# A written table of steps for the 64-wide attention, its value products taken in pairs, its key tiles in reverse

## What is computed

```python
h = _rms(x, ln_w)
q = (h @ wq).reshape(B, S, 32, 64)
k = (h @ wk).reshape(B, S, 8, 64)
v = (h @ wv).reshape(B, S, 8, 64)
q, k = _rope(q, k)
scores = jnp.einsum('bqhd,bkhd->bhqk', q, repeat(k)) / 8.0
scores = jnp.where(causal, scores, -1e30)
attn = jax.nn.softmax(scores, -1)
o = jnp.einsum('bhqk,bkhd->bqhd', attn, repeat(v))
x = x + o @ wo
```

## Time and profile before

| | |
|---|---|
| median of 3 runs | 2234.08 us (2233.0 to 2237.5) |
| profiled execution | 2239.73 us |
| its span in the trace | 2237.9 us |
| PE busy | 1923.3 us, 86% of the span |
| DVE, ACT, POOL busy | 1292.1, 1080.4, 905.6 us |
| 64-wide attention, all rounds | 842 to 1862 us of the span |

### The profile page before, as it was taken

One profiled execution on the slowest core, in us unless ns is written; L12 is line 12 of the kernel. 1 busy time (PEld: TensorE's weight loads), 2 busy tenths in 40 slices (PEclk: granted clock), 3 DMA queues, 4 the chain that ended last, 5 costly groups with the idle time before them and its releaser, 6 DMA issues.

```text
span 2237.9 us, 37392 instructions
## 1 busy us (share of the span) xinstructions
PE 1923.3 (86%) x11178; PEld 1217.4 (54%) x11178; DVE 1292.1 (58%) x3257; ACT 1080.4 (48%) x2758; POOL 905.6 (40%) x1013
## 2 busy tenths in 40 slices
PE   4979899778787739999999999999999996599995
PEld 2656778533333325666666666666666665455552
DVE  5775453457568466666666666666666665822222
ACT  3324342345455416665566556656665663144442
POOL 4990000022120004444444444444444443468884
PEclk9989899769999979999999999999999997799997
DMA  4000020000000100000000000000000003545556
GB/s 143 1 1 1 9 49 1 1 1 1 1 13 26 39 2 1 1 0 0 0 0 0 0 0 0 0 0 0 0 0 0 0 0 111 206 70 82 84 83 160
DMA packets 61350, 60.76 MB, mean 27 GB/s; under 512 B 13136, under 2 KB 58320, under 8 KB 61264
## 3 DMA queue, kind: packets, MB, share of 16 engines
q0 software_dynamic: 15360, 20.98, 5.9%
q1 hardware_dynamic: 45904, 38.65, 5.4%
HBM read 40.48 MB, written 19.14 MB: 27 GB/s over the span
## 4 chain that ended last, share of the span: by engine, by line
PE 62%; DVE 14%; issue 11%; ACT 7%; POOL 4%; DMA 2%; SPq 0%; ACTq 0%; DVEq 0%; POOLq 0%
PE banks L1804 8%; PE banks L1827 7%; PE banks L1836 6%; PE banks L1815 5%; PE banks L1846 4%; PE banks L1900 3%; PE banks L2024 2%; PE banks L1858 2%; ACT wide_x L1468 2%; PE banks L1875 2%; POOL wdT L751 2%; PE banks L1649 2%; ACT wugT L1482 2%; PE banks L1920 2%; PE banks L1942 1%
## 5 line engine op out<-in xcount | busy, mean ns | idle before, releaser
L1051 DVE TENSOR_REDUCE con<-banks 128x1 f32<-128x256 f32 (+3 forms) x512 | 250.3, 489 | 147.9 <-PE banks L1806 141.1
L1804 PE MATMUL banks<-wide_k,wide_q 128*128 128x512 f32 (+3 forms) x1024 | 300.9, 376 | 0.5 <-ACT wide_k L1419 0.5
L683 POOL TENSOR_TENSOR wugT<-wugT,con 128x512 f32<-128x512 f32 (+1 forms) x256 | 237.6, 934 | 134.8 <-DVE con L1041 134.3
L1804 PEld LDWEIGHTS banks<-wide_k,wide_q 128*128 128x128 f32 x1024 | 159.4, 190 | 132.3 <-issue 87.7
L1827 PE MATMUL banks<-attn 128*64 128x256 f32 x1280 | 208.5, 404 | 0.9 <-ACT attn L1447 0.9
L1846 PE MATMUL banks<-late,xnT 128*128 (+1 forms) x512 | 197.2, 508 | 9.7 <-DVE xn L1067 6.3
L1083 DVE TENSOR_REDUCE con<-banks 128x2 f32<-128x1024 f32 x128 | 154.7, 1214 | 66.5 <-PE banks L1888 65.6
L694 POOL TENSOR_TENSOR attn<-attn 128x320 f32<-128x320 f32 x128 | 111.0, 867 | 200.3 <-DVE attn L1029 200.3
L1432 ACT ACTIVATE wugT<-banks,con 128x512 f32<-128x512 f32 (+1 forms) x256 | 161.1, 632 | 58.4 <-DVE con L1051 55.1
L1836 PE MATMUL banks<-late,attn 128*128 (+1 forms) x512 | 141.7, 399 | 28.1 <-DVE attn L1034 25.9
L2024 PE MATMUL banks<-w,late 128*128 x320 | 158.0, 617 | 2.2 <-ACT late L1561 1.7
(11 more groups left out here) (309 smaller groups left out, 4111.6 us busy)
## 6 DMA issues: line engine op xcount, KB each, us to landing
w<-in_L_ffn_w_dram SPq DMA_DIRECT2D x32, 256.0 KB, 6.4
late<-in_L_ffn_w_dram SPq DMA_DIRECT2D x16, 256.0 KB, 6.4
y_rows<-wqkv1T SPq DMA_DIRECT2D x1, 2176.0 KB, 7.9
x<-in_L_attn_x_dram SPq DMA_DIRECT2D x4, 512.0 KB, 9.1
late<-in_L_ffn_wq_dram SPq DMA_DIRECT2D x2, 1024.0 KB, 7.2
late<-in_L_ffn_wo_dram SPq DMA_DIRECT2D x1, 2048.0 KB, 8.3
h_rows<-wugT SPq DMA_DIRECT2D x1, 2048.0 KB, 7.0
y_rows<-x SPq DMA_DIRECT2D x1, 2048.0 KB, 12.8
```

The costliest lines, as they stand in the source:

```text
L683: nc.gpsimd.tensor_tensor(p, p, rinv[:, m:m + 1].to_broadcast([P, n]), ALU.mult).then_inc(at.sem["norm"], 1)
L1051: nc.vector.tensor_reduce(negmax[:, a:a + 1], bank[at.sbank(a)][:, 0:P * at.keys(at.row_of(a))], AX, ALU.max, negate=True).then_inc(at.sem ...
L1804: nc.tensor.matmul(sbank[:, 0:keys], wide_q[:, side, i, qcols], wide_k[:, side, w, 0:keys], start=(w == 0), stop=False)
```

## The change

```diff
-        wide_bufs = shared_buffers(5)
+        wide_bufs = shared_buffers(10)
...
-                rounds = self.stream(4)
-                assert rounds[1] == rounds[2] and len(rounds) == 5
-                self.windows = {"first": [op for op in rounds[0] if (op[0], op[2]) not in sum(late.values(), [])],
-                                "steady": rounds[2], "last": [op for op in rounds[3] if op[1] <= 0], "drain": rounds[4]}
+                steady = [op for slot in range(self.units) for op in [("scores", 0, slot)] + schedule.get(slot, [])]
+                self.windows = {"first": [op for op in steady if op[1] >= 0], "steady": steady,
+                                "last": [op for op in steady if op[1] <= 0], "drain": [op for op in steady if op[1] < 0]}
...
+        def wide_tile(a):
+
+            return TB - 1 - a
...
-        a2 = Attention("a2", [(r, 0) for r in reversed(range(TB))], HD64, True, wide_bufs, 5, 2, 4, 2, 5, WIDE_NEXT, {})
+        a2 = Attention("a2", [(r, 0) for r in reversed(range(TB))], HD64, True, wide_bufs, 10, 2, 2, WIDE)
...
-                if t == 0 and reached(n - 1):
-                    v.wait_ge(at.sem["pv"], (n - 1) * len(at.steps))
+                if reached(n - 1):
+                    v.wait_ge(at.sem["pv"], (n - 2) * len(at.steps) + at.last_step(t) + 1)
...
-                        if reached(n0 + a + 1 - at.n_turned):
-                            v.wait_ge(at.sem["pv"], n0 + a + 1 - at.n_turned)
-                        nc.vector.tensor_copy(at.probsT[:, a % at.n_turned, :], bank[PTBANK[0]][:]).then_inc(at.sem["pt_dve"], 1)
+                        nc.vector.tensor_copy(at.probsT[:, a, :], bank[PTBANK[0]][:]).then_inc(at.sem["pt_dve"], 1)
...
-                            ins = nc.tensor.matmul(bank[YBANK][:, 0:QKV], xnT[:, c, P * a:P * a + P], w_qkv(n, c),
+                            ins = nc.tensor.matmul(bank[YBANK][:, 0:QKV], xnT[:, c, P * wide_tile(a):P * wide_tile(a) + P], w_qkv(n, c),
```

## The result

| | before | after |
|---|---|---|
| median | 2235.8 us (4 runs, 2233.0 to 2238.6) | 2156.6 us (4 runs, 2151.8 to 2160.3) |
| ratio of times | | 0.9644 (95%: 0.9620 to 0.9668) |
| span of the profiled execution | 2237.9 us | 2154.1 us |
| mean steady round | 32.25 us | 29.56 us |
| first round (first scores to the next round's) | 27.1 us | 29.8 us |

The change makes the kernel 3.6% faster. I had forecast 2138 us, 96 us less; it is 79 us less.

The account below looks back on a forecast made before the run. PE was taken to bound the 64-wide attention. 32.26 - 2.5 (waits) - 1.32 (groups) + 0.75 (new waits) = 29.2 us a round; 93 us over 30 rounds plus 3 at the ends gave 2138 us, range 2105 to 2182.

Parts of the forecast that it names:

- What bounds the kernel: In the 64-wide attention PE, busy 95%, sets the pace; only less PE time per step or fewer PE waits help.
- Part 1, the groups: Value steps in six groups instead of ten save entries and ways out on PE: 1.32 us a round.
- Part 2, the waits that go: Six PE waits, at qkv 1, project 2 and 3, turn_qk 0, 2 and 6, go: 2.5 us a round.
- Part 3, the new waits: Three places come out late in the new order, qkv 0, turn_qk 3 and turn_qk 6: 0.75 us a round.
- turn_qk 3: New wait for ACT to empty MBANK of turn_qk 2, with thin cover in slot 9: 0.1 us.
- turn_qk 6: New wait in slot 14 for copy, high parts and low parts queued behind values 3: 0.3 to 0.55, taken as 0.55 us.
- qkv 0: New wait in slot 2 for DVE's add after project 1 in slot 1: about 0.1 us.
- The first and last round: Each has half of the steps, so they save about 3 us together; the drain keeps its steps.
- All waits go: Rival: the three new waits and a smaller one of project 1 vanish; round 28.3 us, 2110 us; chance 0.12.
- The queue behind split: Rival: slow low part 3 delays turn_qk 6 (round 30.2, 2169 us), or pairs don't pay (30.5, 2178 us); chance 0.22.
- Slower: Rival: DVE's maxima fall behind between slots 7 and 13, PE waits for exponentials in each slot; 2253 us; chance 0.06.
- Nothing changes: Rival: something unseen, say a chain around the round's loop through DVE, paces both orders; 2234 us; chance 0.05.

Follow-up runs that it names:

- e5_both: Changed kernel with project 1 moved to the end of slot 0 and split 3 moved ahead of turn 5 in slot 12: round 28.50 us, median 2118.0 us.
- e6_pairs_old: Old order of steps in the new code, with only the value steps regrouped, mostly into pairs: round 30.75 us, median 2186.4 us.
- e1_singles: Changed kernel with four pairs of value steps pulled apart inside the same or the neighbouring slot: round 31.16 us, median 2198.6 us.
- e8_groups: Kernel of e5_both with values in four groups instead of six (0 to 3 in slot 12, 4 to 6 in slot 15): round 28.14 us, median 2108.8 us.
- e2_old_order: Changed kernel's new code with the order of the kernel before in its table: round 32.17 us, median 2233.8 us.
- e3_project0: Changed kernel with project 1 moved from slot 1 to the end of slot 0: round 28.97 us, median 2136.3 us.
- e9_fixed_address: Changed kernel with every qkv multiplying by group 0's block of wqkv, at a constant address: round 29.31 us, median 2144.7 us.
- e11_first_round: Four value groups, steps 0 to 3 in slot 11, both moves of e5_both; first round's preparations in old slots: round 28.50 us, median 2115.3 us.

## Why the prediction was right, point by point

**What bounds the kernel: right.** PE sets the pace; what was taken off the two waits after the change came off the round in full and added up (e5_both). DVE is busy 67% of the changed kernel's stretch.

**Part 1, the groups: right in size.** 1.32 us were priced. The two sides of the test give 1.3 (e6_pairs_old) and, for four pairs pulled apart, 1.1 against 0.95 (e1_singles); e8_groups gave 0.68 against 0.55. One pair in the drain was enough of a row, since every pair in the rounds took 1.01 or 1.02. The Trainium skill states that a change of the tiling mode drains TensorE (TensorEngine Tiling (Array Packing), section "Tiling Modes"), without a price. The trace agrees as far as it goes: 0.18 ahead of a group that follows a turn and 0.15 behind it are what a change costs here, and more steps without a change cost 0.43 each, up to four in a row. That it is a drain, the rows do not show.

**Part 2, the waits that go: right but for one.** Four of the five gaps that were to go are at their marks in the changed kernel, turn_qk 2 among them, so low part 1 was in time. Project 3 kept 0.15 of some 0.6 (0.10 and 0.19 by turns). DVE's copy after qkv 1 still ends last there, by the changed kernel's timeline:

```profile
1266.05 0.21 DVE L1006 COPY attn<-banks 128x64 f32<-128x64 f32 x1
...
1266.41 1.10 PE L1804 MATMUL banks<-late,attn 128*128 x4
```

The prediction had a qkv and the projection two slots later "with over 2 us of PE work between". Between qkv 1 and project 3 it is 1.5 us (from scores 6 at 1264.69 to 1266.22, where project 3 would have started at its mark), and DVE is through with YBANK at 1266.26, 1.1 us after the end of qkv 1.

**Part 3, the new waits: the place right in all three, one size wrong and one small.** turn_qk 3 cost 0.1, as priced. turn_qk 6 cost 0.70 against 0.55 (and against the 0.3 of the lower bound), by the chain that was named: from the start of scores 13 it took 1.87 us (1277.52 to 1279.39) where the walk had 1.75, and PE was there after 1.17 where it had 1.2. qkv 0 was the step that failed: "About 0.1" was 0.56 in the round shown (0.63 from the mask, less 0.07) and 0.64 on average. Of the 0.56, 0.2 was the wait for the add. The walk let the add begin at the projection's end (1.1 + 0.42 = 1.5), and it began 0.17 later, a distance that the earlier trace rows show too. Some 0.3 was register work behind the wait, which no term of the sum had, though the wait in front of a dynamic address could be read in the code.

**Why the round still came close: in part luck.** I summed the distances over their marks in all 30 steady rounds (marks 0.04 and 0.07 as in the prediction, 0.16 ahead of values). Three errors add up to the 0.36 between 29.2 and 29.56:

- The waits after the change are 1.59 us, not 0.75: 0.84 worse.
- The waits before were 2.76 us, not 2.5: project 1 in slot 5 waited 0.18, which I had left out of the sum, and project 2 and 3 waited 0.1 longer in every second round than in the one that I read. 0.27 better.
- The steps themselves, without any wait, fell from 29.50 to 27.97, by 1.53 and not 1.32. 0.21 better.

Without the last two, neither of which was in the sum, the round would have come out at 30.0 us.

**The first and last round: sign wrong for the first.** They were booked at 3 us less; the last round with the drain gave 4.5 and the first took 2.7 more, so 1.8 in all. I had taken the first round for half a steady one, and not looked at its clock. "The drain keeps its steps" was wrong as well: values 6 and project 0 went from the drain into the last round, and the drain became 2.7 us shorter (from the last scores to the last projection 9.35 us before, 6.67 after).

**The sum.** Forecast 96, measured 79 (0.9644 of 2235.8). The rounds gave 81 of the 93, the ends 1.8 of the 3. The unchanged parts gave 1.4 between the two profiled executions, and the medians lie 4.6 us closer together than these two.

**The rivals.** *All waits go* did not come about with this order, but e5_both takes 1.06 us of them away and stands at 28.5, near the 28.3 of that rival. *The queue behind split*: low part 3 took 0.63 and not 1.19, POOL being between two instructions (one ended by 1277.53, the next began at 1279.61), so the slow form played no part in that wait. *Slower*: no gap ahead of scores in the round; three banks held even with slots of 1 us and 3 us. *Nothing changes*: fell with e2_old_order.

## What to carry to other kernels

When one engine is busy 95% of a stretch, read its starts in one round, subtract the tight distances, and write the order out with two slots between each producer chain and its consumer; here fewer waits were worth 1.2 us of a round's 2.7, and putting like matmuls next to each other most of the other 1.5. Before a step is moved to a place where its wait will end last, look at what the engine's sequencer has to do behind that wait: an address from a loop counter cost some 0.3 us there, and nothing where the wait was over 0.35 us earlier (every second round of e3_project0). Moving cover from one wait to another only helps if the resource behind the next wait (here one bank and one engine's fixed list) has slack.

## What the runs showed of the hardware that I had not expected

- Register work for a dynamic address behind a wait that ends last: 0.35 us from release to the first weights, 0.06 with a constant address (e9_fixed_address), 0.05 for project 2 and 3 in e6_pairs_old, where no register work shows behind the wait.
- Products of 64 columns: each further step in a row adds 0.43 us (1.01 for two, 1.45 for three, 1.87 for four); a step by itself 0.58; a turn 0.36 to 0.38 before scores, 0.53 to 0.56 before such a product, 0.59 between two of them.
- In the changed kernel's first round the granted clock fell from 1.00 to 0.50 for about 3 us, in the second of two stretches in which PE was busy 0.92 and 1.37 us of 2. That cost 1.65 us. In e11_first_round and in the kernel before, where PE was busy 1.01 us of 2 in one stretch there and at least 1.7 in its neighbours, it did not fall.
